# Attention kernel: output products of high and low parts, and copies, rotations and scalings in another order

## The reference, cut to what matters

```
qkv = x @ w_qkv                                  # 16 heads of 64
q, k = l2norm(q) * q_scale, l2norm(k) * k_scale
# windows of 128 tokens; each looks at itself and one neighbour on either side
bq = 8 * q;  bq, bk rotated by cos/sin of the position
sim  = einsum('bwid,bwjd->bwij', bq, bk), masked outside the band
attn = softmax(sim);  out = einsum('bwij,bwjd->bwid', attn, bv)
return out @ w_out                               # [1024, 256]
```

## Time and profile before

| | |
|---|---|
| median of 3 runs | 3098.14 us (3097.45 to 3100.73) |
| the profiled execution | 3097.64 us, of which its span 3095.8 us |
| busy share of the span | PE 95%, DVE 76%, ACT 70%, POOL 54% |
| attention stage | from 0 to about 1917 us |
| one sequence in it | 117.3 us |

### The profile page before, as it was taken

How to read it: one execution, slowest core, us unless ns; L and a number is a source line. 1 busy time by engine, 2 the same in 40 slices (tenths; PEclk the granted TensorE clock), 3 DMA queues, 4 the chain that set the end, 5 groups by cost and what they waited for, 6 DMA issues and landing times. The chain is left out here.

```text
span 3095.8 us, 60269 instructions
## 1 busy us (share of the span) xinstructions
PE 2941.9 (95%) x20143; PEld 2332.4 (75%) x20143; DVE 2357.9 (76%) x6845; ACT 2162.1 (70%) x5670; POOL 1662.0 (54%) x2226
## 2 busy tenths in 40 slices
PE   7999999999999999999999996799999999999996
PEld 5777777777777777777777774578888888888885
DVE  6877877877877877877877875787777777777775
ACT  5666766766766766766766764577888888888884
POOL 5655655655655655655655654344555555555555
PEclk9999999999999999999999998899999999999998
DMA  2000000000000000000000002100000000000000
GB/s 84 8 15 22 8 15 22 8 15 22 8 15 17 13 15 15 15 15 15 15 15 15 8 21 64 47 15 8 15 15 15 21 20 16 15 15 15 8 15 21
DMA packets 51218, 57.50 MB, mean 19 GB/s; under 512 B 3008, under 2 KB 48592, under 8 KB 50912
## 3 DMA queue, kind: packets, MB, share of 16 engines
q1 hardware_dynamic: 47904, 50.67, 5.1%
q10 hardware_dynamic: 3008, 2.98, 0.3%
HBM read 36.86 MB, written 16.78 MB: 17 GB/s over the span
## 5 line engine op out<-in xcount | busy, mean ns | idle before, releaser
L627 POOL TENSOR_SCALAR a_ex<-a_ex,a_rc 128x384 f32<-128x384 f32 (+1 forms) x1024 | 533.8, 536 | 691.4 <-DVE a_rc L538 691.2
L433 ACT ACTIVATE a_ex<-a_sm,a_nm 128x384 f32<-128x384 f32 (+1 forms) x1024 | 572.0, 560 | 72.5 <-DVE a_nm L531 61.2
L531 DVE CUSTOM_DVE_ANT_0 a_sm<-sc,a_mask,a_rn 128x384 f32<-128x384 f32 (+1 forms) x1024 | 529.7, 543 | 6.3 <-PE sc L303 6.3
L439 ACT ACTIVATE a_pt<-tp 128x256 f32<-128x256 f32 (+1 forms) x512 | 220.1, 430 | 290.5 <-PE tp L322 290.5
L267 PE MATMUL pj<-a_whi,a_xhi 128*128 128x384 f32 x1024 | 390.3, 381 | 8.8 <-DVE a_wlo L187 5.8
L1695 POOL TENSOR_TENSOR b_alo<-b_ring,b_ahi 128x512 fp32r<-128x512 f32 x128 | 169.6, 1325 | 411.7 <-DVE b_ring L1524 388.0
L611 POOL TENSOR_TENSOR a_qr<-a_ra,a_rb 128x256 f32<-128x256 f32 x512 | 370.5, 739 | 11.2 <-DVE a_rb L511 8.4
L267 PE MATMUL pj<-a_whi,a_xlo 128*128 128x384 f32 x1024 | 347.4, 339 | 0.0
L267 PE MATMUL pj<-a_wlo,a_xhi 128*128 128x384 f32 x1024 | 346.3, 338 | 0.0
L331 PE MATMUL qk<-a_pt,a_v 128*64 128x384 f32 (+1 forms) x2048 | 303.9, 437 | 29.0 <-DVE a_pt L543 26.8
L303 PE MATMUL sc<-a_kT,a_qT 64*64 64x256 f32 (+1 forms) x4096 | 307.6, 415 | 1.6 <-DVE a_nm L531 0.9
(11 more groups left out here) (234 smaller groups left out, 7988.7 us busy)
## 6 DMA issues: line engine op xcount, KB each, us to landing
a_xres<-x SPq DMA_DIRECT2D x16, 512.0 KB, 3.8
y<-a_res SPq DMA_DIRECT2D x16, 512.0 KB, 2.9
b_y<-y SPq DMA_DIRECT2D x16, 512.0 KB, 3.8
a_xin<-x SPq DMA_DIRECT2D x15, 512.0 KB, 3.8
out<-b_y SPq DMA_DIRECT2D x15, 512.0 KB, 2.9
a_xin<-wqkv SPq DMA_DIRECT2D x8, 256.0 KB, 2.7
a_ot<-wqkv ACTq DMA_DIRECT2D x3, 384.0 KB, 9.8
a_stage<-wqkv SPq DMA_DIRECT2D x3, 384.0 KB, 12.3
```

Of the source, the lines that this page charges most:

```text
L433: e.activation(ex[h][w][:, 0:width], sm[h][w % 2][:, 0:width], ACT.Exp, bias=nm[:, w, h:h + 1], scale=-1.0, accum_out=rs[:, w, h:h + 1]).t ...
L439: e.activation(pt_window(0, w), blocks(TP, w), ACT.Copy).then_inc(g['pt_act'], 1)
L531: e.tensor_tensor_reduce(out=sm[h][w % 2][:, 0:width], in0=SC[w % 2][h][:, 0:width], in1=mem['mask'][:, off:off + width], scale=rn[:, par, ...
L627: e.tensor_scalar(row, row, 0.0, rc[:, w, h:h + 1], ALU.add, ALU.mult).then_inc(g['exn_pool'], 1)
```

## The change

It makes the output products of three F32R products (high and low parts of the rows and of `w_out`) in place of one fp32 product; ScalarE's copy gives the high part, VectorE subtracts it from the bank for the low part. q's copy goes from VectorE to ScalarE, placed ahead of the exponentials. The exponential is taken in place (buffers `sm` go). The value products wait in two steps. For the last window of a `spare` pair, VectorE's two copies and a rotation come ahead of the last mask, and its exponential, reciprocal and scaling move to the next half. `dve_stats` of p1, `norm.rstd` and `norm.apply` are moved later. x is loaded straight into the result's buffer, and `w_out` is split in the first sequence (two copies on ScalarE, four subtractions on GpSimd).

```diff
 def pe_values(e, n, p):
-    e.wait_ge(g['pt_act'], NW * n + NW)
-    e.wait_ge(g['pt_dve'], NW * n + NW)
     for k in range(NW):
         lo, hi, width = span(k)
+        if k in (0, 2):
+            e.wait_ge(g['pt_act'], NW * n + NW - 1 + k // 2)
+            e.wait_ge(g['pt_dve'], NW * n + (NW if k or spare(NW * n + NW - 1) else NW - 1))
...
 def pe_out_project(e, seq, k):
...
         for c in range(HC):
-            last = e.matmul(QK[:, t * DIM:(t + 1) * DIM], ot[:, c, (2 * k + t) * P:(2 * k + t + 1) * P],
-                wo[:, c, :], start=c == 0, stop=c == HC - 1)
+            for j, (rows_t, weight) in enumerate(((ohi, wo_hi), (olo, wo_hi), (ohi, wo_lo))):
+                last = e.matmul(QK[:, t * DIM:(t + 1) * DIM], rows_t[:, c, tokens], weight[:, c, :],
+                    start=c == 0 and j == 0, stop=c == HC - 1 and j == 2)
...
 def pe_half(e, at):
...
         if u == 0:
-            if at.has_pair(1):
-                pe_q_transpose(e, n, n + 1, (p + 1) % 2)
             pe_transpose_weights(e, i, w, 0, at.has_next())
             if at.has_pair(2):
                 pe_project(e, seq, n + 2, pair, w, 0)
+            if at.has_pair(1):
+                pe_q_transpose(e, n, n + 1, (p + 1) % 2)
+            if at.has_pair(2):
                 pe_project(e, seq, n + 2, pair, w, 1)
             pe_transpose_weights(e, i, w, 1, at.has_next())
+            pe_transpose_weights(e, i + 1, w + 1, 0, at.has_next())
             if at.has_pair(1):
                 pe_k_transpose(e, n + 1, (p + 1) % 2)
-            pe_transpose_weights(e, i + 1, w + 1, 0, at.has_next())
             pe_transpose_weights(e, i + 1, w + 1, 1, at.has_next())
...
+def act_q_evacuate(e, m, par):
+    e.wait_ge(g['qt_pe'], m + 1)
+    e.activation(qT[par][:, :], QK[:, :], ACT.Copy).then_inc(g['qt_act'], 1)
...
 def act_half(e, at):
...
-            if at.at(2, 0) and not at.first:
-                norm.apply(e, at.b - 1, mem['res'])
+            if i and spare(i - 1):
+                act_exp(e, i + 1, w + 1, 1)
             if at.has_pair(-1):
                 act_o_evacuate(e, n - 1, (p - 1) % PAIRS)
             if at.has_pair(1):
                 act_norms(e, n + 1, (p + 1) % 2)
+            act_evacuate_weights(e, i, w)
+            if at.has_pair(1):
+                act_q_evacuate(e, n + 1, (p + 1) % 2)
             if ahead:
                 act_exp(e, next_i, next_w, 0)
-            act_evacuate_weights(e, i, w)
-            if ahead:
-                act_exp(e, next_i, next_w, 1)
-                act_exp(e, next_i + 1, next_w + 1, 0)
             if at.has_pair(2):
                 act_project(e, n + 2, (p + 2) % PAIRS, w)
             if at.has_pair(1):
                 act_k_evacuate(e, n + 1, (p + 1) % 2)
+            if ahead:
+                act_exp(e, next_i, next_w, 1)
             act_evacuate_weights(e, i + 1, w + 1)
             if ahead:
+                act_exp(e, next_i + 1, next_w + 1, 0)
                 act_exp(e, next_i + 1, next_w + 1, 1)
+            if at.at(2, 0) and not at.first:
+                norm.apply(e, at.b - 1, mem['res'])
         else:
...
             if ahead:
                 act_exp(e, next_i, next_w, 0)
+            if at.has_pair(2):
+                act_project(e, n + 2, (p + 2) % PAIRS, w)
+            if ahead:
                 act_exp(e, next_i, next_w, 1)
                 act_exp(e, next_i + 1, next_w + 1, 0)
             act_evacuate_weights(e, i + 1, w + 1)
-            if ahead:
+            if ahead and not spare(i + 1):
                 act_exp(e, next_i + 1, next_w + 1, 1)
-            if at.has_pair(2):
-                act_project(e, n + 2, (p + 2) % PAIRS, w)
...
-def dve_q_evacuate(e, m, par):
-    e.wait_ge(g['qt_pe'], m + 1)
-    e.tensor_copy(qT[par][:, :], QK[:, :]).then_inc(g['qt_dve'], 1)
+def dve_o_low(e, n, p):
+    e.wait_ge(g['ot_act'], n + 1)
+    e.tensor_tensor(olo[:, p, :], QK[:, :], ohi[:, p, :].bitcast(F32), ALU.subtract).then_inc(g['ol_dve'], 1)
...
 def dve_half(e, at):
...
-        if not at.first:
-            if at.at(1, 0):
-                dve_stats(e, at.b - 1, 1)
+        if u == 0 and at.has_pair(-1):
+            dve_o_low(e, n - 1, (p - 1) % PAIRS)
...
-        if u == 0 and at.has_pair(1):
-            dve_q_evacuate(e, n + 1, (p + 1) % 2)
...
+        if ahead and u == 1 and spare(i + 1):
+            dve_evacuate_weights(e, i + 1, w + 1)
+            if at.has_pair(2):
+                dve_rotate(e, n + 2, w)
             dve_mask_max(e, next_i + 1, par, next_w + 1, 1)
             dve_reciprocals(e, next_i, next_w)
...
+        else:
+            if ahead:
+                dve_mask_max(e, next_i + 1, par, next_w + 1, 1)
+                dve_reciprocals(e, next_i, next_w)
...
+            dve_evacuate_weights(e, i + 1, w + 1)
+            if u == 0 and at.has_pair(2):
+                dve_rotate(e, n + 2, w)
+            if ahead:
+                dve_reciprocals(e, next_i + 1, next_w + 1)
+            if u == 1 and at.has_pair(2):
+                dve_rotate(e, n + 2, w)
+        if at.at(1, 0) and not at.first:
+            dve_stats(e, at.b - 1, 1)
```

More of the change, by code:

```diff
@@ L167, in run_attention, with dma_out_weights, act_out_weights, pool_out_weights @@
     w_in = [nc.alloc_semaphore(f'att_w_in{k}') for k in range(len(PIECES))]
-    w_raw = [mem['stage'][:, :], flat(mem['ot'])[:, 0:3 * HD]]
+    w_raw = [mem['raw'][:, c, :] for c in range(DC)]
     def piece_columns(k):
         return slice(PIECES[k][0] * 3 * PW, (PIECES[k][-1] + 1) * 3 * PW)
-    RAW_UNDER = {0: 3, 3: 4, 4: 5}
+    wo_raw = flat(mem['res'])
+    wo_split = [t[:, :, :].rearrange('p c n -> p (c n)') for t in (wo_hi, wo_lo)]
+    def dma_out_weights(e, k):
+        e.dma_start(mem['res'][:, :, :], io['wo0'].rearrange('(c p) n -> p c n', p=P)[:,
+            4 * k:4 * k + 4, :]).then_inc(g['wo_in'], 16)
+    def act_out_weights(e, k):
+        e.wait_ge(g['wo_in'], 16 * (k + 1))
+        e.activation(wo_split[0][:, k * 1024:(k + 1) * 1024], wo_raw, ACT.Copy).then_inc(g['wo_act'], 1)
+    def pool_out_weights(e, k, part):
+        e.wait_ge(g['wo_act'], k + 1)
+        cols = slice(k * 1024 + part * 512, k * 1024 + (part + 1) * 512)
+        e.tensor_tensor(wo_split[1][:, cols], wo_raw[:, part * 512:(part + 1) * 512],
+            wo_split[0][:, cols].bitcast(F32), ALU.subtract).then_inc(g['wo_pool'], 1)
     x_first = [nc.alloc_semaphore(f'att_x_first{k}') for k in range(2)]
@@ L560, in dve_amax @@
         col = TT * seq + t
-        e.tensor_reduce(mem['amax'][:, col:col + 1], mem['res'][:, t, :], AX.X, ALU.max, apply_absolute_value=True)
+        last = e.tensor_reduce(mem['amax'][:, col:col + 1], mem['res'][:, t, :], AX.X, ALU.max,
+            apply_absolute_value=True)
+        if t == TT - 1:
+            last.then_inc(g['am_dve'], 1)
     def dve_half(e, at):
@@ L568, in dve_half @@
             dve_rotate(e, n + 1, 3)
+        if u == 0 and i and spare(i - 1):
+            dve_reciprocals(e, i + 1, w + 1)
+        if u == 0 and at.has_pair(1):
             dve_norms(e, n + 1)
@@ L637, in pool_half @@
             pool_rotate(e, n + 1, (p + 1) % 2, 3)
+        if u == 0 and i and spare(i - 1):
+            pool_softmax(e, i + 1, w + 1)
+        if u == 0 and at.has_pair(1):
             pool_k_norm(e, n + 1, (p + 1) % 2)
@@ L640, in pool_half @@
             pool_rotate(e, n + 2, p % 2, 1)
-        if at.has_next():
+        if at.has_next() and u == 1 and spare(i + 1):
+            if at.has_pair(2):
+                pool_rotate(e, n + 2, p % 2, w)
             pool_softmax(e, at.next_window, at.next_w)
-            pool_softmax(e, at.next_window + 1, at.next_w + 1)
-        if at.has_pair(2):
-            pool_rotate(e, n + 2, p % 2, w)
-        if at.at(1, 0) and not at.first:
+        else:
+            if at.has_next():
+                pool_softmax(e, at.next_window, at.next_w)
+                pool_softmax(e, at.next_window + 1, at.next_w + 1)
+            if at.has_pair(2):
+                pool_rotate(e, n + 2, p % 2, w)
+        if at.at(1, 1) and not at.first:
             norm.rstd(e, at.b - 1)
@@ L649, in pool_half @@
             pool_weights_low(e, 3 + p // 2)
+        if at.first and p in (4, 6):
+            pool_out_weights(e, p // 6, u)
         if w1_piece(at) is not None:
@@ L736, in _ @@
             act_norms(e, 0, 0)
-            for t in range(TT - 1):
+            for t in range(2):
                 act_project(e, 1, 1, t)
+            act_q_evacuate(e, 0, 0)
+            act_project(e, 1, 1, 2)
             act_k_evacuate(e, 0, 0)
@@ L760, in _ @@
                 dve_rotate(e, 1, t)
-            dve_q_evacuate(e, 0, 0)
             dve_weights_low(e, 2)
@@ L800, in sb @@
         return stack.enter_context(nc.sbuf_tensor('a_' + name, shape, dt))
-    mem = {k: sb(k, v) for k, v in dict(scales=[P, 2, DH], rot=[P, TT, 4, DH], stage=[P, 3 * HD], wo=[P, HC, DIM],
```

(9 more changed lines are left out.)

75 lines of the change are left out of this document (40 added, 35 removed).

## The result

| | before | after |
|---|---|---|
| median | 3098.46 us (3097.45 to 3100.73, 4 runs) | 3145.32 us (3143.27 to 3148.9, 4 runs) |
| the profiled execution | 3097.64 us, span 3095.8 | 3148.9 us, span 3147.1 |
| sequence in the middle | 117.29 us | 120.53 us |

The changed kernel is slower: ratio 1.0148, 95% interval 1.0133 to 1.0163, 47 us by the medians and 51 by the profiled executions. The forecast was 3142, within 3065 to 3165.

What follows compares the result with a forecast made beforehand. PE's stream, busy 114.20 of 117.29 us a sequence, was taken as the bound. 42.6 over 15 sequences, +3.5 and +1.5 in the first, -2.6 and +0.65 in the last: about +45 on 3097.64, 3142 us, range 3065 to 3165.

Steps and rivals of the forecast that it cites:

- Output products: On PE's path, a call falls from 7.01 to 5.68 us; 32 calls save 42.5 us, taken as 41.
- The 56: Output products' saving in us if three passes cost 3/4 of fp32's four, 5.26 a call; not used for the sum.
- The new chain: First half, k's transposes to next scores: chain 2.65 us against 1.94 of PE work, so PE waits 0.71 a pair.
- What it wins: Waits ahead of value products (0.2 to 0.5) and at head 1's transposes (0.23 to 0.3) go; usual pair 12.90 us.
- Normalization: Moved normalization makes PE wait 1.1 us in p1; in p2 1.8 for the mask and about 0.3 for k's scaling.
- p6 and p7: ScalarE's earlier projection copies in p6 delay norms and p7's q transposes: p6 14.1 us (+0.6), p7 13.6.
- The sum: A sequence gains +5.4 us less 2.56 for output products, +2.8; over 15 sequences 42.6, about +45 in all.
- the first sequence and the last: First: +3.5 us, and 1.5 for splitting `w_out`; last: two calls save 2.6, and one waits 0.65.
- the rival without a gain of the products: Output projection calls return to 7 us: +41, 3181 us; included in the 0.06 chance of over 3165.
- VectorE's 91.82: VectorE's busy us in one 117.29 us sequence of the kernel before, as the prediction read it.
- the stall is hidden: Rival: window 1's weights copy comes in time for the scores, 0.71 x 125 = 89 us less, 3053; chance 0.2.
- the end of 3080 to 3112 for an absorbed normalization: Rival: p1's and p2's normalization costs are absorbed but the stall stays, 3097 us, within 3080 to 3112; chance 0.14.

Runs made afterwards that it cites:

- experiment 5: Changed kernel with one fp32 product in place of the three F32R ones in the output projection, low parts left out of the product: 3185.97 us, ratio 1.0277.
- experiment 10: Changed kernel with the edits of Experiment 3, Experiment 4, experiment 5 and experiment 6 together: 3106.03 us, ratio 1.0026 to the kernel before.
- Experiment 1: Changed kernel with VectorE's copy of window 1's weights ahead of window 2's reciprocal in every first half: 3132.29 us, ratio 1.0101.
- experiment 6: Changed kernel with ScalarE's second exponential of window 2 ahead of k's copy in the first half of a pair: 3116.29 us, ratio 1.0051.
- Experiment 3: Changed kernel with the first normalization's statistics, rstd and apply all put back in their old places: 3111.09 us, ratio 1.0038.
- Experiment 4: Changed kernel with ScalarE's projection copies in p6's second half put back behind the exponentials: 3135.69 us, ratio 1.0115.
- experiment 9: Changed kernel with the edits of Experiment 1, Experiment 3, Experiment 4 and experiment 6 together: 3068.37 us, ratio 0.9904 to the kernel before.

## Why the prediction was right, point by point

- **Output products.** A call takes 5.85 us, where I had 5.68: the first of the 48 takes 0.23 to the next start, the others 0.120 and not 0.118. By the starts the term is 37 and not 41; experiments 5 and 10, by their medians, measured 41 and 38. The Trainium skill ("FP8 and Floating Point Precision", TensorE Precision Notes) gives four passes for true fp32. That a reduced product takes a single one is my reading; the Trainium skill says there only that its operand is truncated. The 56 worked out from both would overstate the gain: three products of the kind took 5.85 us against 7.01, a ratio of 0.83 and not 3/4.
- **The new chain.** 2.65 us of chain against 1.94 of work was forecast, 2.64 against 2.01 came: 0.63 us of wait instead of 0.71. The chain was right to 0.01, PE's own work beside it 0.07 short. Experiments 1 and 6 cut the chain at two different links; the one removes the stall, the other all but 17 of its 82 us.
- **What it wins.** Waits ahead of the value products gone (29.0 to 0.6 us), as said. The usual pair came out at 12.87 and 12.88 instead of 12.90.
- **Normalization.** In p1 PE waits 1.05 us for the mask (1.1 forecast). In p2 it waits 0.39 for k's scaling (0.3) and 1.55 for the mask (1.8). Experiment 3 prices the two at 34 us, where 2.9 a sequence would be 43; the old places have a cost too: in experiment 3 PE waits 0.36 us at q's transposes of p2 and 0.40 for a mask of p1.
- **p6 and p7.** 14.14 and 13.61 for 14.1 and 13.6. Experiment 4 shows the cause for p7, 10 us. For p6 the number was right and the reason given was not: with the copies put back it takes 14.18. It has the usual stall (0.62 us) and keeps its wait for the mask (0.22, and 0.23 before), where I had let that wait go and counted on the copies.
- **The sum.** +3.24 a sequence instead of +2.8, of which p1, p2 and p0 give 0.47. Over 15 sequences 49 us; the stage ends 49 us later, so the first sequence and the last balance, where I had +3. The stage behind it took 2 us more. That 3142 lies within 4 us of the median is in part luck: 0.47 a sequence too little is made up by the 3 us too much. The sum as written gives 3143, not 3142, and the rival without a gain of the products 3183, not 3181; nothing hangs on either, nor on VectorE's 91.82, which is 91.80 in the earlier trace rows.
- **Where the text was wrong though the number held.** The rival "the stall is hidden" was priced at 0.71 x 125 = 89 us. The stall can be removed, and it brought 13 and 29 us. It was not an independent term: the mask behind it is nearly as late, at a moment that ScalarE's queue sets (experiment 9), and its slack came from the stall. Had the forecast been on that rival's side, 3053 would have been 60 us off. Conversely the end of 3080 to 3112 for an absorbed normalization was just met, by experiment 3's 3111.

## What to carry to other kernels

Idle time ahead of one instruction is not what its removal brings; what the next instruction on that engine waits for has to be read first, and here a 65 to 80 us stall was worth 13 to 29. Five kernels brought the mask at the same moment, since none of their orders took work out of the queue that sets it. Steps that belong to one chain over several engines (statistics, rstd, apply) have to be moved or put back together, since one of them alone gave +17 us where all three gave -34. And a change that bundles a gain with a reordering is worth taking apart: some 40 us of gain and three placements that cost 77 together made a kernel 47 us slower, and without them it is 30 us faster.
